# Scores of the first attention from split halves: three reduced-precision passes in place of one fp32 matmul, single buffers for the split x, and x's lower half first on the POOL engine

## The reference, cut to what matters

```python
q = (x @ wq).reshape(B, L, NUM_HEADS, HEAD_DIM)          # 16 heads of 128
k = (x @ wk).reshape(B, L, NUM_KV_HEADS, HEAD_DIM)       # 4 heads of 128
v = (x @ wv).reshape(B, L, NUM_KV_HEADS, HEAD_DIM)
q = rms_norm(q, q_norm_w);  k = rms_norm(k, k_norm_w)
k_ctx = rms_norm((h_ctx_kv @ wk_ctx).reshape(...), k_norm_w);  v_ctx = ...
q = q * cos + rotate_half(q) * sin;  k = k * cos + rotate_half(k) * sin
k_full = jnp.concatenate([k_ctx, k], axis=1);  v_full = ...   # 64 + 512 keys
scores = jnp.einsum('blhd,bmhd->bhlm', q, k_full) * scale + mask
out = jnp.einsum('bhlm,bmhd->blhd', softmax(scores), v_full)
return out.reshape(B, L, -1) @ wo
```

## Time and profile before

| | us |
|---|---|
| runs | 2028.35, 2028.88, 2036.26 |
| the profiled execution | 2035.64 |
| its span | 2033.8 |
| PE busy in the span | 1866.4 (92%) |
| PEld busy | 1335.9 (66%) |
| DVE busy | 1100.0 (54%) |
| ACT busy | 1042.3 (51%) |
| POOL busy | 964.1 (47%) |
| mean granted clock of PE | 0.961 of full speed |

### The profile page before, as it was taken

The page is one execution under the profiler, slowest core; times in us unless marked ns, Lnnn a source line. Parts: engine busy times, 40 slices in busy tenths (PEclk is TensorE's granted clock), DMA queues, the critical chain, the costliest instruction groups (busy, mean ns, idle before and its releaser), DMA issues. The chain is left out here.

```text
span 2033.8 us, 27627 instructions
## 1 busy us (share of the span) xinstructions
PE 1866.4 (92%) x9759; PEld 1335.9 (66%) x9796; DVE 1100.0 (54%) x2266; ACT 1042.3 (51%) x2249; POOL 964.1 (47%) x865
## 2 busy tenths in 40 slices
PE   6999999999999999999997999989999578849998
PEld 4667667776666666676665877769998356624443
DVE  4554444455465554655435458323343578748886
ACT  3555556545554545454543311136565267647775
POOL 4644455444554445544421100038887256537774
PEclk8999999999999999999997899989999789969999
DMA  6111102111121111110004100157889370000000
GB/s 230 49 54 48 37 33 69 38 32 47 33 69 49 49 48 33 49 49 23 1 0 149 47 21 21 42 181 221 233 223 250 102 157 1 1 0 22 17 22 27
DMA packets 112952, 141.18 MB, mean 69 GB/s; under 512 B 37408, under 2 KB 68128, under 8 KB 112624
## 3 DMA queue, kind: packets, MB, share of 16 engines
q1 hardware_dynamic: 105648, 122.63, 19.4%
q0 software_dynamic: 7168, 16.78, 3.9%
HBM read 104.78 MB, written 29.36 MB: 66 GB/s over the span
## 5 line engine op out<-in xcount | busy, mean ns | idle before, releaser
L865 PE MATMUL a_A<-a_pT,a_vf 128*128 128x512 f32 (+1 forms) x448 | 237.0, 611 | 1.4 <-ACT a_pT L549 1.2
L710 POOL TENSOR_TENSOR a_xcl<-xT,a_xch 128x512 fp32r<-128x512 f32 x64 | 82.5, 1289 | 322.7 <-ACT a_xch L533 322.7
L815 PE MATMUL a_S<-a_kT,a_qT 128*128 128x288 f32 (+3 forms) x640 | 209.9, 426 | 4.8 <-ACT a_qT L561 3.1
L626 DVE TENSOR_REDUCE a_nmax<-a_S 128x1 f32<-128x192 f32 (+3 forms) x256 | 138.2, 552 | 85.6 <-PE a_S L816 84.2
L539 ACT ACTIVATE a_pr_odd<-a_S,a_nmax 128x320 f32<-128x320 f32 (+1 forms) x128 | 81.0, 634 | 155.8 <-DVE a_nmax L626 154.6
L120 PE MATMUL a_A<-a_wlo,a_xch 128*128 128x512 f32 x256 | 152.8, 597 | 6.4 <-DVE a_qT L622 6.4
L815 PEld LDWEIGHTS a_S<-a_kT,a_qT 128*128 128x128 f32 x640 | 115.1, 190 | 54.3 <-issue 28.3
L549 ACT ACTIVATE a_pT<-a_TR 128x512 f32<-128x512 f32 (+1 forms) x224 | 132.3, 591 | 35.8 <-PE a_TR L855 35.0
L539 ACT ACTIVATE a_pr_even<-a_S,a_nmax 128x192 f32<-128x192 f32 (+1 forms) x128 | 67.1, 526 | 132.5 <-DVE a_nmax L626 132.4
L1460 POOL TENSOR_TENSOR e_wlo<-expert_raw,e_whi 128x1408 fp32r<-128x1408 f32 x32 | 102.5, 3222 | 68.0 <-ACT e_whi L1533 68.0
L2331 PE MATMUL f_HH<-w12T,f_xqT 128*128 128x512 bf16 x497 | 119.3, 388 | 7.8 <-DVE f_xqT L2283 4.4
(11 more groups left out here) (388 smaller groups left out, 5166.7 us busy)
## 6 DMA issues: line engine op xcount, KB each, us to landing
a_pw<-in_L_ffn_w_dram SPq DMA_DIRECT2D x96, 256.0 KB, 2.8
expert_raw<-in_L_ffn_w_gate_dram SPq DMA_DIRECT2D x16, 704.0 KB, 7.3
expert_raw<-in_L_ffn_w_up_dram SPq DMA_DIRECT2D x16, 704.0 KB, 9.6
expert_raw<-in_L_ffn_w_down_dram SPq DMA_DIRECT2D x16, 512.0 KB, 10.2
tern<-a_tern SPq DMA_DIRECT2D x48, 128.0 KB, 1.9
x_res<-in_x_dram SPq DMA_DIRECT2D x4, 1024.0 KB, 9.2
a_raw<-in_L_xattn_wq_dram SPq DMA_DIRECT2D x4, 1024.0 KB, 6.0
a_raw<-in_L_xattn_wo_dram SPq DMA_DIRECT2D x4, 1024.0 KB, 5.4
```

The source lines that it names most:

```text
L626: ve.tensor_reduce(nmax[:, s % 2, i:i + 1], pair(s, i), AX.X, ALU.max, negate=True).then_inc(s_max, 1)
L710: pool.tensor_tensor(xcl[:, t % 2], xT[:, :, tok(t)], xch[:, t % 2].bitcast(F32), ALU.subtract).then_inc(xlo_ready, 1)
L815: pe.matmul(bank[:, lo:hi], qT[:, t % 2, hq], kT[:, par(t), lo:hi], start=True, stop=hi < nk)
L865: last = pe.matmul(A[:, A_USE["V", t, 0][0]], vf[r, par(t), i], pT[r, i % 2], start=i == 0, stop=i == nkt - 1)
```

## The change

Scores are computed in three passes like the projections. ACT's copies k and t now write fp32r upper halves `kTh` and `qTh`, DVE gets two new steps in every slot, l0 and l1, that subtract them from PSUM into `kTl` (128 x 128) and `qTl` (128 x 512), and the context's keys, which a DMA brought straight to `kT`, go to `kcs` and are split by a step y on ACT and DVE (once per sequence and period). The buffers that this takes are found by halving others: `qTh` and `qTl`, `xch` and `xcl` have one buffer now, so that x of tile s+2 is split in slot s, after the q projection of tile s+1 has read the one before. POOL does x first in every slot, ahead of the weight split w too. The TR bank of a turned q or k is given back by DVE's l step where ACT's copy did it. In slot -1 PE does G0 ahead of k0, and the tanh of the gates is now called m.

```diff
@@ orders
-                -1: "k0 k1 G0 K T R q0 q1 q2 q3",
+                -1: "G0 k0 k1 K T R q0 q1 q2 q3",
@@ ACT_ORDER
-                 -2: "c1 x v h0 f h1",
-                 -1: "x v d0 k t r f y",
+                 -2: "c1 v h0 f h1",
+                 -1: "x d0 v k t r f m y",
-                 2: "w x e0 j0 e1 g0 j1 v e2 r g1 n j2 e3 g2 k t o f",
+                 2: "x w e0 j0 e1 g0 j1 v y e2 r g1 n j2 e3 g2 k t o f",
@@ DVE_ORDER, POOL_ORDER
-    DVE_SLOT = "M0 M1 N0 D X v M2 N1 N2 j0 j1 M3 N3 B E A"
-    DVE_ORDER = {..., -2: "v E A", -1: "v X E A", "first": DVE_SLOT,
+    DVE_SLOT = "M0 M1 N0 D X v M2 N1 N2 y j0 j1 M3 l0 l1 N3 B E A"
+    DVE_ORDER = {..., -2: "v E A", -1: "v X l0 l1 E A y", "first": DVE_SLOT,
-    POOL_ORDER = {-3: "r0 r1 r2 r3 x w c0", -2: "x c1 r", -1: "q x r", "first": "x q p0 p1 r",
-                  0: "x q p0 p1 r", 1: "x q p0 u p1 w r", 2: "w q x p0 p1 r", 3: "x q p0 p1 r"}
+    POOL_ORDER = {-3: "r0 r1 r2 r3 x w c0", -2: "c1 r", -1: "q x r", "first": "x q p0 p1 r",
+                  0: "x q p0 p1 r", 1: "x q p0 u p1 w r", 2: "x q p0 p1 r", 3: "x q p0 p1 r", "change": "x w q p0 p1 r"}
@@ steps
+        kind = s if s < 0 else "first" if s == 0 else "change" if s % PERIOD == PERIOD - 2 and "change" in order else s % BT
@@ buffers
-        xch = s_.sb("xch", [P, 2, KD, P], F32R)
-        xcl = s_.sb("xcl", [P, 2, KD, P], F32R)
+        xch = s_.sb("xch", [P, KD, P], F32R)
+        xcl = s_.sb("xcl", [P, KD, P], F32R)
-        kT = s_.sb("kT", [P, 2, KEYS])
+        kTh, kTl = s_.sb("kTh", [P, 2, KEYS], F32R), s_.sb("kTl", [P, 2, KEYS], F32R)
+        kcs = s_.sb("kcs", [P, T])
-        qT = s_.sb("qT", [P, 2, GH * P])
+        qTh, qTl = s_.sb("qTh", [P, GH * P], F32R), s_.sb("qTl", [P, GH * P], F32R)
@@ ACT
-                    if name == "x" and live(s, 3):
-                        t = s + 3
-                        until(act, q_full, tile, t - 2, m)
+                    if name == "x" and (s == BEGIN or live(s, 2)):
+                        t = 0 if s == BEGIN else s + 2
+                        until(act, q_full, tile, t - 1, m)
@@ DVE
+                    if name == "y" and context(s) is not None:
+                        n = context(s)
+                        ve.wait_ge(ch_ready, n + 1)
+                        ve.tensor_tensor(kTl[:, n % 2, 0:T], kcs[:], kTh[:, n % 2, 0:T].bitcast(F32), ALU.subtract).then_inc(cl_ready, 1)
+                    if name == "l" and live(s, 1):
+                        t = s + 1
+                        if i == 0:
+                            until(ve, kh_ready, tile, t, m)
+                            ve.tensor_tensor(kTl[:, par(t), key_cols(t)], TR[:, TR_USE["K", t, 0][0], 0:P],
+                                             kTh[:, par(t), key_cols(t)].bitcast(F32), ALU.subtract).then_inc(kl_ready, 1)
+                        else:
+                            until(ve, qh_ready, tile, t, m)
+                            ve.tensor_tensor(qTl[:], TR[:, TR_USE["T", t, 0][0]], qTh[:].bitcast(F32), ALU.subtract).then_inc(ql_ready, 1)
@@ PE
-                        sem, count = {"P": (pT_ready, turn(before[2])), "T": (qT_ready, tile), "K": (kT_ready, tile),
+                        sem, count = {"P": (pT_ready, turn(before[2])), "T": (ql_ready, tile), "K": (kl_ready, tile),
-                            until(pe, qT_ready, tile, t, m)
-                            until(pe, kT_ready, tile, t, m)
+                            until(pe, ql_ready, tile, t, m)
+                            until(pe, kl_ready, tile, t, m)
                             if t % BT == 0:
-                                until(pe, ck_loaded, lambda v: 16 * batch(v), t, m)
+                                until(pe, cl_ready, batch, t, m)
-                            pe.matmul(bank[:, lo:hi], qT[:, t % 2, hq], kT[:, par(t), lo:hi], start=True, stop=hi < nk)
+                            mm3(pe, bank[:, lo:hi], qTh[:, hq], qTl[:, hq], kTh[:, par(t), lo:hi], kTl[:, par(t), lo:hi], True, hi < nk)
```

More of the change, by code:

```diff
@@ L172, in steps @@
     def steps(order, s):
-        return [(word[0], int(word[1:] or 0)) for word in order[s if s < 0 else s % BT if s > 0 else "first"].split()]
+        kind = s if s < 0 else "first" if s == 0 else "change" if s % PERIOD == PERIOD - 2 and "change" in order else s % BT
+        return [(word[0], int(word[1:] or 0)) for word in order[kind].split()]
     def batch_next(s):
@@ L180, in row, with context @@
         return i if s == BEGIN else s + ahead if BT <= s + ahead < PERIOD else None
+    def context(s):
+        return 0 if s == -1 else batch_next(s) // BT if s % BT == 2 and live(batch_next(s), 0) else None
     def bank_order(firsts):
@@ L293, in attention0_stage @@
         tern = s_.sb("tern", [P, 2, 512], BF16)
-        below = s_.sb("below", [P, 512], BF16)
+        below = xn[:, 0, 0:256].bitcast(BF16)
         sabs, thr, nthr = s_.sb("sabs", [P, PIECES]), s_.sb("thr", [P, 3]), s_.sb("nthr", [P, 3])
@@ L329, in attention0_stage @@
         pT_ready, o_hi, o_lo, wo_done = (s_.sem(n) for n in ("pT_ready", "o_hi", "o_lo", "wo_done"))
-        qT_ready, kT_ready = s_.sem("qT_ready"), s_.sem("kT_ready")
+        qh_ready, ql_ready, kh_ready, kl_ready, ch_ready, cl_ready = (s_.sem(n) for n in (
+            "qh_ready", "ql_ready", "kh_ready", "kl_ready", "ch_ready", "cl_ready"))
         kv_act, kv_done = s_.sem("kv_act"), s_.sem("kv_done")
@@ L560, in do @@
                         until(act, q_turned, tile, t, m)
-                        act.activation(qT[:, t % 2], TR[:, TR_USE["T", t, 0][0]], ACT.Copy).then_inc(qT_ready, 1)
+                        act.activation(qTh[:], TR[:, TR_USE["T", t, 0][0]], ACT.Copy).then_inc(qh_ready, 1)
                     if name == "v" and live(s, 2):
@@ L706, in do @@
                                                    ALU.subtract).then_inc(wlo_ready, 1)
-                    if name == "x" and live(s, 3):
-                        t = s + 3
+                    if name == "x" and (s == BEGIN or live(s, 2)):
+                        t = 0 if s == BEGIN else s + 2
                         until(pool, xhi_ready, tile, t, m)
-                        pool.tensor_tensor(xcl[:, t % 2], xT[:, :, tok(t)], xch[:, t % 2].bitcast(F32), ALU.subtract).then_inc(xlo_ready, 1)
+                        pool.tensor_tensor(xcl[:], xT[:, :, tok(t)], xch[:].bitcast(F32), ALU.subtract).then_inc(xlo_ready, 1)
                     if name == "q" and live(s, 1):
@@ L834, in do @@
                         for k in (2 * i, 2 * i + 1):
-                            last = mm3(pe, bank, xch[:, t % 2, k], xcl[:, t % 2, k], wkvh[:, k], wkvl[:, k], k == 0, k == KD - 1)
+                            last = mm3(pe, bank, xch[:, k], xcl[:, k], wkvh[:, k], wkvl[:, k], k == 0, k == KD - 1)
                         if i == 1:
@@ L842, in do @@
                             until(pe, wlo_ready, chunk(0, i), t, m)
-                        last = mm3(pe, A[:, A_USE["q", t, 0][0]], xch[:, t % 2, i], xcl[:, t % 2, i], whi[:, 0, i], wlo[:, 0, i],
+                        last = mm3(pe, A[:, A_USE["q", t, 0][0]], xch[:, i], xcl[:, i], whi[:, 0, i], wlo[:, 0, i],
                                    i == 0, i == KD - 1)
```

24 lines of the change are left out of this document (14 added, 10 removed).

## The result

| | before | after |
|---|---|---|
| runs, median us | 2029.45 (4; 2028.35 to 2036.26) | 2044.21 (4; 2043.57 to 2045.72) |
| the profiled execution | 2035.64 | 2044.13 |
| its span | 2033.8 | 2042.4 |
| last W3 of the first attention starts at | 1079.2 | 1088.1 |
| PE busy | 1866.4 | 1854.7 |

The ratio is 1.0067 (95% interval 1.0044 to 1.0090). The kernel before was run again beside the experiments; over all 42 runs its median is 2031.8, so the change costs about 12 us (15 against the four runs in the table). The two profiled executions lie only 8.5 apart, since that of before was one of its slower runs. Up to the last W3 of the first attention the changed kernel is 8.9 late, and behind it nothing is added.

What follows compares the result with a forecast made beforehand. PE's own work was taken to set the pace in the first attention. Terms of -26.6, +9.3, +7.5, +15.0, +0.5 and +1.5 sum to +7.2 on the median 2028.88: 2036 us, range 2016 to 2075.

Steps and rivals of the forecast that it cites:

- PE's work in the scores: Three fp32r passes instead of fp32 scores on PE save 1.66 us a sequence, -26.6 us over 16 sequences.
- prologue, slots 0 and 1, clock: New waits of K, R, S0 and k0 up to slot 1, +9.3 us; a stretch at half clock, +1.5.
- slots 2 to 10: k0 waits for POOL's x in every slot, 0.6 to 1.8 us each, 9.6 in all, net +7.5.
- slots 11 to 61: Later DVE steps l0 and l1 and POOL's x make S0, W0, T and K wait: +15.0 us, forecast for slots 11 to 63.
- behind: The last slots of the first attention, +0.5 us.
- rows 5: Profile rows: four fp32 turnings with 128 moving columns take 0.43 us, none closer than 0.108; used to price 192-column passes.
- the narrow rival: Scores: a 192-column fp32r pass costs as much as an fp32 matmul, +41 us, time 2074; chance 22% with its like.
- my marks 0.22 and 0.18: Distance in us from first to last of three 192-column rows: 0.22 means the price is right, 0.18 too dear.
- 27 us less as a sign: PE's busy time in the span was to fall by about 27 us.
- In other slots l1 ends in time: Slots 11 on, other slots: l1 delays nothing; only W0 waits, 0.1 and 0.08 us in 13 slots each, 2.3.
- Cover: Rival: the forecast waits mostly don't come, and 192-column passes may cost 0.088; 2024 us, at best 2012; chance 20%.
- The passes dearer than read by 0.02: Rival: each new operand load costs more at 192, 320 and 448 columns, +0.02 us on 960 passes, +19 us.

Runs made afterwards that it cites:

- experiment 3: The changed kernel with A (the layer norm's statistics) ahead of E in every slot on DVE: 2034.33 us, 1.0015 of before.
- experiment 10: The kernel before (fp32 scores, two buffers of x) with the mended tables of experiment 8 as far as they apply and its own slot -1: 2004.66 us, 0.9859.
- experiment 8: The changed kernel with the order tables of DVE, ACT and POOL mended slot by slot: 1988.32 us, 0.9782 of before.
- experiments 7 to 10: Besides experiment 8 and experiment 10: changed kernel with slot -1, A, N3 and side work reordered, 2007.88 us; experiment 8 with fp32 scores, 2012.44 us.

## Why the prediction was right, point by point

Forecast and traces, in us (slot starts are S0's; the scores' saving, 1.44 a sequence, is taken out of each stretch):

| term | forecast | measured |
|---|---|---|
| PE's work in the scores | -26.6 | -23.0 |
| prologue, slots 0 and 1, clock | +9.3 and +1.5 | +9.1 |
| slots 2 to 10 | +7.5 | +7.7 |
| slots 11 to 61 | +15.0 | +16.3 |
| behind | +0.5 | -1.1 |
| sum | +7.2 | +9.0 (8.9 unrounded) |

- *The scores.* A pass of 192 columns costs 0.11, like a turning in the earlier trace rows, and a head 0.32, not 0.26 as by its columns alone: the price that I read from rows 5 held and the narrow rival fell. The slots with 192 keys gain nothing. (From the first to the last of the three rows it is 0.20, between my marks 0.22 and 0.18; the third step, to the mask matmul, is 0.12.) The slots without new waits gained 0.31 (slot 13, with its 0.1 at W0 taken out), 0.49 (slot 22) and 0.64 (slot 11), where I had 0.40, 0.56 and 0.72. The term is oversized by a seventh: a head takes 0.09, 0.13 and 0.18 less, close to the 0.10, 0.14 and 0.18 that I had, but what follows its mask matmul starts 0.01 to 0.02 later behind it than before.
- *PE's busy time.* I named 27 us less as a sign, and it fell by 11.7. Up to the end of the first attention (1079.4 and 1088.5) it fell by 17.0, from 1035.1 to 1018.2. Behind that it is 5.3 longer, but there the trace of before has 36 matmul records fewer for the same instructions, so part of these 5.3 is missing records. In slots 11 to 61 the passes save 18.2 and busy time falls by 14.0; W0's waits in the slots with 192 keys, 13 x 0.30 = 3.9, lie mostly inside the mask matmul's record. Ahead of S0 of slot 0 busy time rises by 2.4, with the slower products there.
- *The prologue.* K was at 45.08 (forecast 45.4), R waited 0.74 (1.3), S0 for y 4.08 (4.1), k0 of slot 1 3.89 (4.1). That K came out is luck: xcl was ready at 42.24 and not 43.91, and the twelve products behind it took 2.69 at half clock and not 1.44. The half clock came as feared: the q projections of slot -1 ran at it as far as 50.96, and a good part of slot 0 as well, where before had 1.00. Little was added by it: slot 0 took 12.85 with it against 12.22, since the slower products fill time in which PE had waited 1.4 for POOL and DVE, and in slot 1 the wait of k0 ends when POOL is done. So the prologue and slots 0 and 1 took 9.1, and not 9.3 and 1.5 more.

```profile
core 0: us, PE busy (x) PEld busy (x) DVE busy (x) ACT busy (x) POOL busy (x), PEclk, DMA share, GB/s
42.39:50.96 8.57, 7.83 (x28) 6.79 (x29) 1.83 (x5) 1.81 (x5) 0.00 (x0) 0.50 0.01 3
56.40:64.00 7.60, 7.60 (x27) 5.75 (x28) 1.72 (x6) 1.47 (x6) 6.06 (x7) 0.68 0.00 0
```

- *Slots 2 to 10.* Nine waits of k0, 8.4 us, the longest 1.3; the price was right, and experiment 3 showed the cause.
- *Slots 11 on.* The new waits by step: S0 +4.0, T +2.9, K +2.0, and W0, counted from the mask matmul to W0 so that short ones hidden in the tail of a record are seen, +6.1: 15.0 in sum, as forecast, but not distributed as forecast (the table's 16.3 holds 1.3 more, which is not accounted for). W0 in the 13 slots with 192 keys waits 0.30 each, not 0.08. The step that was wrong is "In other slots l1 ends in time": it does for S0, but l1 starts with ACT's copy and pushes N3 and B behind it. All instructions of line 693 from 235 to 1058 us, and what ended DVE's idle time ahead of them:

```profile
L693 DVE TENSOR_TENSOR a_otl<-a_A,a_oth x52: 678/684/693, 237.8 to 1045.3; 128x512 fp32r<-128x512 f32 x52
its engine sat idle before it (us, times) until:
  ACT a_oth L567: 22.6, 13
```

Before, ACT's upper half ended DVE's idle time ahead of this step 49 times out of 52; now 13 times, and in the other 39 DVE comes to it without a pause. That the sum still came out is in part luck, here as in the whole: the passes brought 3.6 less than forecast and slots 11 on cost 1.3 more, while the prologue with the clock cost 1.7 less and the last slots 1.6 less.
- *The runs.* On the medians I said 2036 and 2044 was measured, within the range. Of the 8 us missed, 2.9 are that the median of before's three runs (2028.88) lay under that of 42 (2031.8); 3.8 that its profiled execution (2035.64) lay over it, where that of the changed kernel lies on its own median; and 1.3 the sum (8.5 between the two profiled executions, against 7.2).
- *The rivals.* Cover: the waits were all there. The passes dearer than read by 0.02: each was within 0.01. I gave slower than by 0.5% a chance of 0.42; the measured ratio is 0.67%, its interval from 0.44.

## What to carry to other kernels

When the busiest engine is made faster in a pipeline with hand-written orders, count first what stands ahead of each operand that it will now ask for earlier, and mend those orders with the change: here the same three passes were worth 12 us or 19 us in slots 11 to 61, by the orders around them (15 or 24 in the runs), and moving the side work behind a row maximum brought 17. A buffer halved to make room puts the split that fills it into the same slot as its use; whoever is ahead of it in that engine's queue is then on the path. And a wait's length is no price: the 9 us earlier start of slot 0 brought 1 to 4.

## What the runs showed that I had not expected

- The kernel before itself held 22 of the 27 us of experiment 10 in the orders of its first attention, though PE was busy for 98% of its stretch from slot 11 on. DVE's busy share of about a half doesn't tell that 2.6 us of side work stand ahead of a row maximum: they cost PE by their place.
- The same wait can cost more in one slot than in the next. In the changed kernel PE waits 2.4 us for S0 in slot 34 and again in slot 50, with much the same waits behind it (T 1.3 in both), and slot 34 takes 1.2 us longer: its first 3 us run at a granted clock of 0.50. In the kernel before, with a wait of 1.55 ahead of both, it was slot 50 that had the lower clock (0.91 on average, 18.42 us) and slot 34 that had not (16.91).

```profile
600.61:618.45 17.84, 16.53 (x76) 11.82 (x76) 10.96 (x26) 7.68 (x20) 7.22 (x7) 0.90 0.24 77
857.67:874.35 16.68, 15.17 (x76) 10.77 (x76) 11.06 (x26) 7.58 (x20) 7.23 (x7) 1.00 0.20 55
```

- In experiment 8 some 8 us of the gain lie behind the start of slot 62 (7.4 in the traces): 2.1 in the last slots of the attention, and nearly all of the rest where nothing was changed. From the last `a_otl` to the first product of the experts' stage it took 272 us in the traces of experiments 7 to 10 and 277 in the changed kernel (275 before), with the same instructions. Two stretches of nearly the same work, which ran at granted clocks of 0.88 and 0.94 in the changed kernel, ran at 0.92 and 1.00 in experiment 8:

```profile
1129.00:1169.00 40.00, 40.00 (x221) 34.05 (x221) 19.29 (x43) 9.87 (x18) 5.24 (x8) 0.88 0.14 53
1169.00:1209.00 40.00, 40.00 (x160) 30.79 (x160) 15.99 (x36) 8.47 (x10) 0.00 (x0) 0.94 0.07 27
```
```profile
1079.00:1119.00 40.00, 40.00 (x228) 34.01 (x228) 19.52 (x43) 10.40 (x19) 5.25 (x8) 0.92 0.15 56
1119.00:1159.00 40.00, 39.22 (x167) 30.32 (x166) 16.96 (x41) 8.65 (x11) 0.00 (x0) 1.00 0.07 27
```

Whether this faster stretch follows from how the attention ends or differs from run to run was not settled; the spread of before's own runs, 2028 to 2036, is of the same size.
